# Squaring the layer-norm input on ScalarE instead of VectorE in a fused attention and feed-forward kernel

## What is computed

```python
def _qlora_linear(x, q, scale, bias, la, lb):
    w = _dequant(q, scale)
    base = jnp.einsum('btd,od->bto', x, w) + bias
    lora = jnp.einsum('btr,or->bto', jnp.einsum('btd,rd->btr', x, la), lb)
    return base + lora

h = x
for blk in range(3):
    i0, i1 = (2 * blk, 2 * blk + 1)
    y = _qlora_linear(h, qweights[i0], scales[i0], biases[i0], lora_a[i0], lora_b[i0])
    y = _layernorm(y, ln_gamma[blk], ln_beta[blk])
    y = jax.nn.gelu(y, approximate=False)
    y = _qlora_linear(y, qweights[i1], scales[i1], biases[i1], lora_a[i1], lora_b[i1])
    h = y + h
return h
```

## Time and profile before

| | |
|---|---|
| median of 2 runs | 4080.87 us (4072.41 to 4089.32) |
| the profiled execution | 4079.71 us |
| its span, first to last instruction on the slowest core | 4078.2 us |
| spans of the 8 cores | 4065.7 to 4078.2 us |
| mean granted clock of PE, by core | 0.747 to 0.751 |
| busy: PE, DVE, ACT | 2512.5, 1983.0, 1082.5 us |

### The profile page before, as it was taken

How to read it: one execution, slowest core, us unless ns; L and a number is a source line. 1 busy time by engine, 2 the same in 40 slices (tenths; PEclk the granted TensorE clock), 3 DMA queues, 4 the chain that set the end, 5 groups by cost and what they waited for, 6 DMA issues and landing times.

```text
span 4078.2 us, 57687 instructions; the slowest of 8 cores (4065.7 to 4078.2 us)
## 1 busy us (share of the span) xinstructions
PE 2512.5 (62%) x20176; PEld 1598.3 (39%) x20176; DVE 1983.0 (49%) x3863; ACT 1082.5 (27%) x1825; POOL 88.4 (2%) x142
## 2 busy tenths in 40 slices
PE   0466665566656566666534857668485666758575
PEld 0344443444434344444302534435353434435343
DVE  1455544455544454555323555455455554545454
ACT  0122233322223322223364212222121222212122
POOL 1000000000000000000020000000000000000000
PEclk9776765677776667676556878878697888879787
DMA  9011111111111111111232010010102010010101
GB/s 139 14 35 27 25 34 30 30 29 30 31 25 30 31 33 30 30 32 24 31 106 64 1 52 1 21 32 5 48 1 52 1 30 23 6 47 1 47 1 32
DMA packets 259707, 128.20 MB, mean 31 GB/s; under 512 B 229232, under 2 KB 233504, under 8 KB 259424
## 3 DMA queue, kind: packets, MB, share of 16 engines
q1 hardware_dynamic: 224512, 62.94, 8.7%
q0 software_dynamic: 34912, 61.57, 6.9%
HBM read 61.99 MB, written 25.17 MB: 21 GB/s over the span
## 4 chain that ended last, share of the span: by engine, by line
PE 41%; DVE 28%; ACT 10%; issue 9%; DMA 5%; DVEq 2%; another core or an unknown queue 2%; SPq 1%; ACTq 1%; POOLq 0%; POOL 0%
PE psA L1276 8%; PE psB L1461 5%; PE psA L1461 4%; DMA arena<-arena 4%; ACT arena L796 3%; PE psA L774 3%; DVE arena L1402 2%; DVE arena L1396 2%; PE psA L386 2%; PE psA L461 2%; DVE arena L808 2%; DVE arena L1302 2%; DVE arena L1382 2%; PE psA L1282 2%
## 5 line engine op out<-in xcount | busy, mean ns | idle before, releaser
L1276 PE MATMUL psA<-arena,wbig 128*128 128x256 bf16 x3072 | 482.7, 310 | 50.1 <-DVEq L1305 50.1
L1276 PEld LDWEIGHTS psA<-arena,wbig 128*128 128x128 bf16 x3072 | 302.7, 109 | 172.8 <-issue 86.0
L774 PE MATMUL psA<-arena 64*128 64x256 bf16 x960 | 250.1, 389 | 169.9 <-ACT arena L796 167.4
L808 DVE TENSOR_TENSOR arena<-arena,mlocS 128x512 bf16<-128x512 bf16 x480 | 204.1, 425 | 228.1 <-ACT arena L796 203.2
L1302 DVE TENSOR_SCALAR arena<-psA,biasS 128x256 bf16<-128x256 f32 x384 | 185.8, 484 | 243.9 <-PE psA L1282 194.0
L1363 ACT ACT_TABLE_LOAD x48 | 61.6, 1283 | 861.0 <-DVEq L1356 861.0
L796 ACT ACTIVATE arena<-psA 128x512 bf16<-128x512 f32 x480 | 262.5, 595 | 58.3 <-PE psA L774 54.5
L1461 PE MATMUL psA<-arena,wbig 128*128 128x256 bf16 x1536 | 222.2, 293 | 0.0
L386 PE MATMUL psA<-wbig,arena 128*128 128x512 bf16 x512 | 137.3, 430 | 129.1 <-DMA arena<-arena 120.2
L547 ACT ACT_TABLE_LOAD x16 | 20.5, 1283 | 688.6 <-PE psC L477 688.6
L1461 PE MATMUL psB<-arena,wbig 128*128 128x256 bf16 x1536 | 202.4, 275 | 0.0
(11 more groups left out here) (169 smaller groups left out, 4437.5 us busy)
## 6 DMA issues: line engine op xcount, KB each, us to landing
y<-arena POOLq DMA_DIRECT2D x16, 1024.0 KB, 4.4
arena<-qT POOLq DMA_DIRECT2D x48, 256.0 KB, 2.6
arena<-x_in POOLq DMA_DIRECT2D x16, 512.0 KB, 7.2
x2scr<-arena SPq DMA_DIRECT2D x16, 512.0 KB, 3.1
arena<-x2scr POOLq DMA_DIRECT2D x16, 512.0 KB, 6.6
arena<-arena SPq DMA_TRANSPOSE x224, 3.2
wbig<-wq POOLq DMA_DIRECT2D x1, 2048.0 KB, 17.4
wbig<-wk POOLq DMA_DIRECT2D x1, 2048.0 KB, 29.3
```

Of the source, the lines that this page charges most:

```text
L774: mm = t.matmul(reg[:, hh * 256:(hh + 1) * 256], ar_t.ap()[0:64, o_KR + h * 2 * W + sl * W + koff: o_KR + h * 2 * W + sl * W + koff + 128] ...
L808: v.tensor_tensor(dst.rearrange("p (g q) -> p g q", g=2), dst.rearrange("p (g q) -> p g q", g=2), mkv, op=ALU.mult)
L1276: t.matmul(reg, wTv(i0, c, oc * 128, 128), V(hin_o + c * TILE, TILE), start=(c == 0), stop=False)
```

## The change

In b_L1e the square goes from DVE to ACT as an activation of the function Square, still one operation over 2048 columns; it waits for the last evacuation by ev1, and PE's L1330 waits for it on sc instead of ve. The placeholder Sqrt goes from b_Ga into the same ACT program, behind the Square. In the loop b_Ga is called ahead of b_L1e where both stand in a step. Lines behind the first edit have other numbers in the new kernel by one: L1310, L1421 and so on of before become L1311 (Square) and L1312 (placeholder); L1345, L1363 and L1374 become L1346, L1364 and L1375; L1416 becomes L1417, and L1433, L1444, L1461 and L1467 become L1432, L1443, L1460 and L1466.

```diff
@@ b_L1e
-            @block.vector
-            def _(v, y1o=y1o, sqo=sqo):
-                v.tensor_tensor(V(sqo, NCH * TILE), V(y1o, NCH * TILE),
-                                V(y1o, NCH * TILE), op=ALU.mult)
-                I(ve, v.drain())
-            st['sq_ve'] = ve.n
+            @block.scalar
+            def _(s, y1o=y1o, sqo=sqo, sro=st['srow']):
+                s.wait_ge(ev1.h, st['y1_evac'])
+                I(sc, s.activation(V(sqo, NCH * TILE), V(y1o, NCH * TILE), AF.Square))
+                I(sc, s.activation(ar_t.ap()[0:1, sro + 4 * TILE:sro + 4 * TILE + 1],
+                                   onesS[0:1, 0:1], AF.Sqrt))
+            st['sq_sc'] = sc.n - 1
@@ b_L1m
-                t.wait_ge(ve.h, st['sq_ve'])
+                t.wait_ge(sc.h, st['sq_sc'])
@@ b_Ga
                 st['g_done'] = sc.n
-                I(sc, s.activation(ar_t.ap()[0:1, sro + 4 * TILE:sro + 4 * TILE + 1],
-                                   onesS[0:1, 0:1], AF.Sqrt))
@@ the loop over pairs, tile A
                     b_Y1b(Bst, k)
                     b_L2(A, k)
+                    b_Ga(A, k)
                     b_L1e(Bst, k)
                 else:
                     b_L2(A, k)
+                    b_Ga(A, k)
                 if k == 1 and 2 * pair + 2 < nbt_total:
                     emit_x2load(2 * pair + 2)
-                b_Ga(A, k)
@@ the loop over pairs, tile B
                     b_Y1b(A, k + 1)
                     b_L2(Bst, k)
+                    b_Ga(Bst, k)
                     b_L1e(A, k + 1)
                 else:
                     b_L2(Bst, k)
+                    b_Ga(Bst, k)
                     b_tail(A)
-                b_Ga(Bst, k)
```

## The result

The changed kernel takes 4034.88 us in the median of 27 runs, against 4083.6 us of before in 26 runs beside them. The ratio is 0.9875, with a 95% interval of 0.9845 to 0.9906: 51 us less, between 38 and 63. The forecast was 4026.8 us and 52.9 us less. The medians themselves are 49 us apart, since some executions run with a lower granted clock on a part of the chip (13 of the 27 took 4018 to 4027 us, the others up to 4097) and the ratio leaves out the slowest of these on both sides. The two lowest times, 4072.4 and 4018.3 us, are 54.1 us apart.

What follows compares the result with a forecast made beforehand. No engine was full; a chain walking between engines bounded the kernel, with the square queued ahead of copies PE awaits. 43.2 + 10.8 - 1.1 = 52.9 us less than 4079.7 gave 4026.8 us, range 4006 to 4056 us.

Steps and rivals of the forecast that it cites:

- Kind 1: 32 places where the square delays the Y2 copy that PE's L1467 awaits; 1.35 us each, 43.2 us gained.
- Kind 2: 8 places, layer 0: tile A's square delays tile B's copy L1255, awaited at L1282; 10.8 us gained.
- Kind 3: 8 places, tile B's layer-0 square before tile A's L1v: ScalarE's square delays L1363 by 0.14 us; 1.1 us lost.
- The Square: Duration of the 2048-column activation on ScalarE, estimated at 1.91 us, bounds 1.23 and 2.11 us.
- One load for its block: ScalarE's block of Square and Sqrt loads one table; two would cost 10.2 us more at pair starts.
- The placeholder: Sqrt on ScalarE loads a table, yet L1363 loads again; saves nothing, so moving it loses nothing.
- The rule of the Trainium skill: Multiplications belong on VectorE, as faster; judged by that alone the moved squares would be 94 us dearer.
- The clock: Share of long, low-clock steps (11 of 32) stays; zero, bounds 16 us gained to 27 us lost.
- A: PE waits as much longer at L1374 as the copy comes sooner; 4079.7 us, chance 0.04.
- B: ScalarE ends last at the pair's start, through a dearer Square or two loads; 4039 us with both, chance 0.08.
- C: Clock stays low in uncovered groups behind the wait at L1276; 36 us slower, 4116 us, chance 0.03.
- D: Larger gain by clean steps throughout; 4011 us, chance 0.04 including beyond.

Runs made afterwards that it cites:

- e8_kind1_only: Changed kernel with layer 0's squares back on VectorE, only those of layers 1 and 2 on ScalarE; ratio 0.990 to the kernel before.
- e6_act_twice: Changed kernel with the Square done twice in a row on ScalarE; ratio 0.992 to the kernel before.
- e7_no_placeholder: Kernel before with the placeholder Sqrt (L1421) left out; lowest run 4077.0 us, that of before beside it 4075.7.
- e1_dve_behind: Kernel before, square kept on VectorE but queued behind the copy (second one at a pair's start unmoved); ratio 0.987 to the kernel before.
- e2_one_block: Changed kernel with Square and real square root in one ScalarE program, no placeholder; ratio 0.978 to the kernel before.
- e5_dve_twice: Kernel before with the square done twice in a row on VectorE; ratio 1.0255 to the kernel before.
- e9_fill: e2_one_block with 18 unread matmuls added ahead of the fifth group in 32 steps; ratio 0.966 to the kernel before.
- e4_placeholder_l1v: Kernel before with the placeholder Sqrt moved into L1v's ScalarE program, ahead of its wait; ratio 0.987 to the kernel before.

## Why the prediction was right

*Kind 1* (43.2 us). Right in place and size. The copy starts 0.19 us after the last evacuation, the wait went from 1.44 to 0.1 us; e8_kind1_only has 41 us for it, and the steps of core 5 have 46.4. The 3.2 us above the term are the clock's: from the fifth group on they have 36.8 us at the lower level for 42.3, an estimated 2.7 us of time, one long step fewer included.

*Kind 2* (10.8 us). Right: L1282's wait is gone, and e8_kind1_only brings it back (10.0 us in the 7 of 8 that are named). The stretches between pairs, which have kinds 2 and 3, lost 1.14 us each for 1.35 - 0.14 = 1.21 reckoned.

*Kind 3* (1.1 us lost). Right that DVE's 0.85 us would not arrive; the price was 0.02 us a time and not 0.14, since the placeholder took 0.19 us and started 0.1 us ahead of the Square's end. e6_act_twice shows that these 8 places are the only bare ones: a second Square of 1.91 us made the wait at the broadcast 2.0 us longer there and nowhere else.

*The Square* (1.91 us): 1910 ns. *One load for its block*: so it is, 48 loads at L1311, each of 1.28 us and with the Square 0.01 us behind it. The drain that the Trainium skill adds to a load ("ScalarE: Activation LUTs", What ACT_TABLE_LOAD costs) does not show here either.

*The placeholder*: worth nothing in its old place, as the trace of before said; e7_no_placeholder shows it.

*The rule of the Trainium skill* ("ScalarE: Activation LUTs", Rules for kernel authors: multiply on VectorE) is right on the durations, 1226 ns on VectorE and 1910 on ScalarE, but not on the kernel's time: the work became dearer, and the kernel faster. The 94 us that the prediction reckoned for it were too many even as work, since the load is not added but comes in place of the placeholder's: ACT is busy 85 us more and DVE 58 less. e1_dve_behind is what the rule and the order of the queue give together: with the square on VectorE behind the copy it costs nothing there either, and the kernel gains as much.

*The clock* (zero, from 16 gained to 27 lost). The share of long steps stayed, 10 and 9 of 32 on core 5, so the term was near zero. Nothing in the prediction gave a reason why it should stay: that was luck. What I did not see is that changing a wait can move the low clock. A step has two long ones, at L1374 and at L1276; the low groups behind the first are covered by the second, those behind the second by nothing. The change took away a wait behind which the clock had stayed high. In e2_one_block and e5_dve_twice the same reckoning, waits times count, missed by half and by 1.6 times. In the changed kernel alone the error could not show.

*The rivals.* A fell: L1375's waits are 163.9 us by 163.0. B's place was right and its price was not: ACT does end last at a pair's start (its load for L1364 starts at 2675.87, 0.93 us behind the end of DVE's part), but with one load and 1.91 us that costs next to nothing. C fell in this kernel, though e5_dve_twice shows its mechanism at work, with the wait lengthened rather than moved. D fell: long steps did not vanish.

*The size.* 4026.8 by 4034.9 measured, 8 us apart. The 52.9 us lie inside the measured 38 to 63, and the lowest runs are 54.1 us apart. Core 5, with 57.4, has 4.5 us more than the sum; the difference is in its clock terms, in the first steps of a pair (3 us) and in the steps of kind 1 (3 us), less 1.7 us in kinds 2 and 3, of which these rows hold 7 of the 8 places.

## What to carry to other kernels

Before work is moved to another engine, look at what stands behind it in its queue: if that is what someone waits for, putting it a place later in the same queue may bring as much, as it did here. A term worked out as a wait times its count holds for TensorE only while the clock behind it stays as it was; where waits of several us follow each other, ask which of the slow groups lie under a later wait and which will after the change. A placeholder that is to load a table early must stand in the same program block as the activation it serves.

## What was not expected of the hardware

- Where the low clock falls in a step of some 30 us depends on the waits, but not on the length of the last one alone. 8 matmuls took 1.05 us behind the waits of 1.44 us (before, L1467), and up to 1.89 us behind those of 2.80 us (e5_dve_twice) and 3.48 us (e2_one_block, granted clock 0.57). Behind a wait of 1.7 us both were seen: 1.00 in the step of e2_one_block and 0.58 in that of e9_fill. What decides between them stays open. Filling the wait of 3.48 us with 18 unneeded matmuls (2.14 us) left no low clock in the groups behind it (0.0 us on core 2, for 95.3 us in e2_one_block on core 5) and made the kernel 49 us faster.
- Table loads are placed anew in each program block: 48 loads of 1283 ns at L1364, a Sqrt, each with a Sqrt as the activation ahead of it. In one block with a wait between the two activations the second load is not there (e2_one_block, e4_placeholder_l1v).
- A one-column activation behind the activation of 2048 columns started 0.09 us before its end (2726.72 by 2724.90 + 1.91).
